# A Swin-style window attention block on one core: the copy of v split in two, and the narrow low parts of norm 2 moved ahead of the second half of the scores

## The reference, cut to what matters

```python
xn = layernorm(x, ln1_w, ln1_b)
xs = jnp.roll(xn, shift=(-3, -3), axis=(1, 2))          # shifted 7x7 windows, no mask
qkv = windows(xs) @ qkv_w + qkv_b                       # 6 heads of 32, 49 tokens a window
attn = softmax((q @ k.T) * hd ** -0.5)
x = x + unwindow((attn @ v) @ proj_w + proj_b)
h = layernorm(x, ln2_w, ln2_b)
h = gelu(h @ mlp_w1 + mlp_b1, approximate=False)        # 192 -> 768
x = x + (h @ mlp_w2 + mlp_b2)                           # 768 -> 192
```

## Time and profile before

| | value |
|---|---|
| median of the timed runs | 3025.48 us |
| the profiled execution, its own time | 3029.68 us |
| its span, first to last instruction | 3027.8 us |
| mean granted clock of TensorE, share of full speed | 0.995 |
| TensorE busy | 2994.0 us (99%) |
| weight loads busy | 2832.8 us (94%) |
| VectorE busy | 2376.4 us (78%) |
| ScalarE busy | 2302.3 us (76%) |
| GpSimd busy | 1672.7 us (55%) |

### The profile page before, as it was taken

How to read it: one execution, slowest core, us unless ns; L and a number is a source line. 1 busy time by engine, 2 the same in 40 slices (tenths; PEclk the granted TensorE clock), 3 DMA queues, 4 the chain that set the end, 5 groups by cost and what they waited for, 6 DMA issues and landing times.

```text
span 3027.8 us, 114959 instructions
## 1 busy us (share of the span) xinstructions
PE 2994.0 (99%) x43446; PEld 2832.8 (94%) x43446; DVE 2376.4 (78%) x6418; ACT 2302.3 (76%) x4493; POOL 1672.7 (55%) x1934
## 2 busy tenths in 40 slices
PE   7999999999999999999999999999999999999998
PEld 6999999999999999999999999999999999999997
DVE  5887888788778877887788788878877887788775
ACT  4777777777777777777777777777777777777776
POOL 3555555555555555555555555555555555555553
PEclk8999999999999999999999999999999999999999
DMA  1110001001100100010001000100110010001000
GB/s 47 28 29 25 24 26 29 24 24 27 29 24 24 29 26 24 24 30 26 24 25 30 25 24 26 29 24 24 27 29 24 24 29 26 24 24 30 26 25 18
DMA packets 109326, 79.79 MB, mean 26 GB/s; under 512 B 7294, under 2 KB 108782, under 8 KB 109294
## 3 DMA queue, kind: packets, MB, share of 16 engines
q1 hardware_dynamic: 107682, 77.18, 9.4%
q10 hardware_dynamic: 1612, 2.16, 0.2%
HBM read 40.78 MB, written 38.54 MB: 26 GB/s over the span
## 4 chain that ended last, share of the span: by engine, by line
PE 98%; DVE 1%; ACTq 1%; ACT 0%; issue 0%; POOL 0%; DVEq 0%; POOLq 0%
PE ps L836 36%; PE ps L839 16%; PE ps L913 6%; PE ps L945 5%; PE ps L867 5%; PE ps L918 5%; PE ps L964 5%; PE ps L919 4%; PE ps L914 4%; PE ps L915 4%; PE ps L799 3%; PE ps L807 2%; PE ps L929 2%; PE ps L933 1%; PE ps L809 1%
## 5 line engine op out<-in xcount | busy, mean ns | idle before, releaser
L390 POOL TENSOR_TENSOR gl<-g,gh 128x392 fp32r<-128x392 f32 x768 | 788.4, 1049 | 251.1 <-ACT gh L684 250.3
L836 PE MATMUL ps<-zh,w 128*128 128x392 f32 x3072 | 722.7, 350 | 0.6 <-ACT zh L646 0.6
L836 PEld LDWEIGHTS ps<-zh,w 128*128 128x128 f32 x3072 | 532.8, 188 | 65.3 <-ACT vt L672 39.8
L275 POOL TENSOR_TENSOR prob<-prob,rcp 128x588 f32<-128x588 f32 x128 | 152.6, 1192 | 529.6 <-DVE rcp L575 529.6
L424 DVE BATCH_NORM_STATS2 st<-xin 98x6 f32<-98x192 f32 x512 | 145.9, 348 | 321.8 <-DMA xin<-in_x 321.6
L678 ACT ACTIVATE g<-ps,biasf 128x392 f32<-128x392 f32 x768 | 389.9, 575 | 2.9 <-PE ps L836 2.9
L363 POOL TENSOR_TENSOR xb<-xin,projbv 98x768 f32<-98x768 f32 x128 | 234.8, 1834 | 271.3 <-DVE z L437 265.2
L684 ACT ACTIVATE gh<-g 128x392 fp32r<-128x392 f32 x768 | 364.6, 533 | 0.0
L836 PE MATMUL ps<-zh1c,wqkv 128*128 128x392 f32 x1536 | 360.9, 343 | 2.6 <-DVE zh1c L447 2.6
L696 ACT ACTIVATE yn<-ps,cols 64x392 f32<-64x392 f32 x128 | 74.9, 585 | 281.2 <-PE ps L919 281.2
L913 PE MATMUL ps<-gh,w2h 128*128 128x392 f32 x768 | 287.7, 375 | 0.2 <-ACT pt L761 0.2
(11 more groups left out here) (110 smaller groups left out, 7290.8 us busy)
## 6 DMA issues: line engine op xcount, KB each, us to landing
xin<-in_x SPq DMA_DIRECT2D x128, 147.0 KB
out<-yo SPq DMA_DIRECT2D x128, 147.0 KB
xin<-in_x SPq DMA_DIRECT2D x128, 71.2 KB
out<-yo SPq DMA_DIRECT2D x128, 71.2 KB
xin<-in_x SPq DMA_DIRECT2D x128, 54.8 KB
out<-yo SPq DMA_DIRECT2D x128, 54.8 KB
xin<-in_x SPq DMA_DIRECT2D x128, 18.8 KB
out<-yo SPq DMA_DIRECT2D x128, 18.8 KB
```

The source lines that it names most:

```text
L390: pool.tensor_tensor(gl[:, m, :], g[:, m, :], gh[:, m, :].bitcast(F32), ALU.subtract)\
L836: last = pe.matmul(dst, cols(w, part), act_, start=(n == 0), stop=(n == 4))
```

## The change

Three things are done.

- The one copy of v from two PSUM banks (L672, 768 columns) becomes two copies of one bank each (384 columns). The first stands ahead of the first exponential, the second between the two exponentials, where the whole copy stood. The matmuls of v signal each bank when it is ready.
- Chunk 2 of `mlp1` waits for the first copy alone, and chunk 3 for the second. The other users of `v_done` and `v_ready` count two where they counted one.
- On VectorE, `low_narrow2` goes from behind `scores(i, 1)` to ahead of it, straight behind `low_wide2`.

```diff
             def pad_windows(grp):
-                wait(pool, v_done, 1, grp - 1, 1)
+                wait(pool, v_done, 2, grp - 1, 2)
...
                 if feeds(i):
                     low_wide2(prev)
+                    low_narrow2(prev)
                 if attends(i):
                     scores(i, 1)
-                if feeds(i):
-                    low_narrow2(prev)
...
-            def values(i):
+            def values(i, pairs):
-                wait(act, v_done, 1, i, 1)
+                wait(act, v_done, 2, i, pairs + 1)
                 wait(act, pv_done, 1, i - 1, 1)
-                act.activation(vt[:, :, :], ps[0:PAIR + 1, V:V + 2, :].rearrange("p b (q n) -> p (b q) n", n=256)[:, :, 0:C],
+                act.activation(vt[:, 2 * pairs:2 * pairs + 2, :],
+                               ps[0:PAIR + 1, V + pairs, :].rearrange("p (q n) -> p q n", n=256)[:, :, 0:C],
                                ACT.Copy).then_inc(v_ready, 1)
...
                 if attends(i):
+                    values(i, 0)
                     exponential(i, 0)
-                    values(i)
+                    values(i, 1)
                     exponential(i, 1)
...
-                last.then_inc(v_done, 1)
+                    if p % 2:
+                        last.then_inc(v_done, 1)
...
-                    if m == 2 and attends(prev + 1):
-                        wait(pe, v_ready, 1, prev + 1, 1)
+                    if m >= 2 and attends(prev + 1):
+                        wait(pe, v_ready, 2, prev + 1, m - 1)
...
             def turn_probs(i):
-                wait(pe, v_ready, 1, i, 1)
+                wait(pe, v_ready, 2, i, 2)
```

## The result

The changed kernel takes 3098.61 us (median of 4 runs, 3097.75 to 3098.9), the kernel before 3025.22 us (median of 4, 3024.63 to 3027.86): a ratio of 1.0237, 95% interval 1.0224 to 1.0250. It is slower by 73.4 us. Between the two profiled executions the difference is 3098.62 - 3029.68 = 68.9 us, since the one of before lies 4.5 us above its median; what follows from the traces is to be held against 68.9, or 0.543 us in each of the 127 bodies.

What follows compares the result with a forecast made beforehand. TensorE was taken as the bound, beside a loop through three engines: a 0.88 us delay less 0.23 us slack gives +0.65 us in each of 127 bodies, about +83 us on 3025.5, so 3108 us; range 3079 to 3115.

Steps and rivals of the forecast that it cites:

- The copy of v hidden, each half 0.5 us: ScalarE, around the first exponential: two copies of 0.5 us cost nothing, hidden in idle time; at most 0.2 us otherwise.
- TensorE's two stops gone, 0.40 us: `mlp1`: stops ahead of chunk 2 (0.25 us) and passes 3 and 4 (0.15 us) go; TensorE reaches `turn_probs` 0.40 us earlier.
- the wait in half 1 alone: TensorE's transposes: half 1 (L945), due at about 1503.39, waits for GELU until 1503.65.
- The second subtraction and exponential 0.88 us later: VectorE, then ScalarE: the moved narrow pair delays `scores(i, 1)` and the second exponential by 0.88 us, the high end.
- My low bound of 0.65: VectorE: if the moved pair overlaps its neighbours, the scores shift by 0.65 us, giving 3079 us.
- ScalarE's chain has 0.23 us of slack there: At the MLP's first output matmul (L913): it could have started at 1504.36 but started at 1504.59.
- each as soon as the one in front is done: ScalarE, second exponential to copies of the transposed probabilities: each instruction starts once its predecessor ends, with no idle time.
- All move by 0.88 us: ScalarE behind the second exponential: table load, GELUs, high parts and copies of the probabilities are all 0.88 us later.
- my 0.05 us: From the end of ScalarE's first copy of the probabilities to L913: a released instruction starts 0.03 to 0.05 us later.
- Rival (a), faster: ScalarE's chain not delayed; TensorE's 0.40 us gain cut to the 0.23 us slack: 29 us gained, 2996 us; chance 0.09.
- Rival (c), part of the delay made up between exponential and copies: ScalarE makes up about 0.3 us of the delay, so 44 us slower, 3070 us; chance 0.07.
- Rival (d), the attention output late for `proj`: Ahead of L774, 0.05 us left isn't enough: a further 0.1 to 0.2 us a body, 3121 to 3134 us; chance 0.07.

Runs made afterwards that it cites:

- e2: Changed kernel with `low_narrow2` put back behind `scores(i, 1)`, so only the copy of v is split: 3024.30 us, ratio 0.9998 to the kernel before.
- e4: Changed kernel with both narrow low parts kept in partitions 0 to 63 and written to a scratch tile: 3050.31 us, ratio 1.0084 to the kernel before.
- e5: Kernel before with v's copy split and `mlp1` passes 0 to 2 of chunk 5 moved ahead, narrow parts unmoved: 2984.95 us, ratio 0.9865.
- e6: Kernel before with only `mlp1` passes 0 to 2 of chunk 5 moved ahead, v copied by one instruction: 3011.62 us, ratio 0.9953.
- e1: Kernel before with only `low_narrow2` moved ahead of `scores(i, 1)`, v copied by one instruction: 3095.46 us, ratio 1.0235.
- e3: Changed kernel with the second narrow low part put back behind the second half of the scores: 3047.76 us, ratio 1.0074 to the kernel before.
- e7: Changed kernel with `mlp1` passes 0 to 2 of chunk 5 moved ahead: 3099.18 us, ratio 1.0241 to the kernel before.

## Why the prediction was right, and which term was off

The forecast was 3108 us, +83; measured is +73.4 (+68.9 between the profiled executions). Step by step:

- The copy of v hidden, each half 0.5 us: right, 0.49 us in ScalarE's idle time. The first exponential starts at 7.94 us from the residual, before at 7.85; nobody waits for it, as the prediction had it. e2 shows that the split is free.
- TensorE's two stops gone, 0.40 us: right, it was 0.37. L947 starts at 13.90 us from the residual, before at 13.98. It would have started at 13.61 (0.36 us behind the last pair at 1511.46), but its weight load waits 0.46 us there. I had expected the wait in half 1 alone; it is in both halves, since GELU of chunk 1 is late as well. It costs nothing, as L915 is later still.
- The second subtraction and exponential 0.88 us later: right to the hundredth. The reason, that L461 neither overlaps its neighbours nor is overlapped, was shown in e4, which got 0.36 of the 0.88 back. My low bound of 0.65 was too high, by the overlap inside the pair.
- "ScalarE's chain has 0.23 us of slack there": this is the term that was mis-sized; it was 0.88 - 0.54 = 0.34. The step behind it is "each as soon as the one in front is done", and with it "All move by 0.88 us". Three things were wrong in it. The first copy didn't start as soon as the one in front was done: it waited for TensorE, worth 0.17 us when TensorE is early. Each copy took 0.662 us (median) before and 0.634 after, 0.03 less. And the way from the copy's end to the matmul is longer than my 0.05 us: 1513.74 + 0.63 = 1514.37 to 1514.51, 0.14, so 0.09 us of the slack wasn't there. The rows held a sign of this: the narrow parts end at 1499.36 and the passes that need them start at 1499.51, 0.15 later. 0.23 + 0.17 + 0.03 - 0.09 = 0.34. With it the sum is 127 x 0.54 = 69, against 68.9 between the profiled executions. Here 0.09 of the error in the slack hid part of the other 0.20; without it the forecast would have been further off. e5 and e4 agree with the larger slack: in e5 L917 is 0.36 us earlier where 0.23 would have allowed 29 us of gain, not 42, and e4's shift of 0.52 costs 25 us where 0.23 would give 127 x 0.29 = 37.
- The remaining 4.5 us between 68.9 and 73.4 is the distance of the profiled execution of before to its median. The prediction took 4.2 us off, as if the changed kernel's profiled execution would also lie above its median; it lies on it (3098.62 and 3098.61). So in terms of the profiled executions the forecast was 3113 against 3098.6, 14 us too high (127 x 0.11), and it is luck that only 9 of them are left between the medians.
- Rival (a), faster: e5 has its condition, a shift of 0 with both stops gone, though reached by another edit, and gains 42 us where the rival said 29. By the traces the change would have lost nothing below a shift of about 0.34 us (0.23 in the prediction); no run has a shift between 0 and 0.48.
- Rival (c), part of the delay made up between exponential and copies: part of it was true. Of the 0.88 us, 0.17 are made up there, not 0.3, and not because ScalarE works faster but because a gap in its chain closes; the prediction had held against it that "the rows join without a gap".
- Rival (d), the attention output late for `proj`: not seen; ScalarE still waits for TensorE ahead of L775 in 62 bodies (12.9 us), so it is nearly level, as the prediction had it.

## What to carry to other kernels

When a stop of the busiest engine is removed by reordering its supplier, follow what is pushed back on the supplier until it meets the busy engine again, and compare that delay with the slack at the meeting point; here 0.88 us against 0.34 at a place 6 us further on. It can be cheaper to give the waiting engine other work that is ready than to hurry what it waits for. And a slack read off a trace can hide the waiting engine's own lateness: ask of each instruction in the chain whether it starts by overlapping the one in front or after a gap.

## What the runs showed of the hardware

- Two VectorE instructions of 64x196 elements that read one half of the partitions and write the other take 0.76 us from the first's start to the next instruction; two of the same size that stay in partitions 0 to 63, and write to a tile of their own, take 0.54 us: they overlap each other and the next (e4).
- A copy of 128x588 from PSUM by ScalarE took 0.660 to 0.662 us (median of 256) in the kernel before, in e2 and in e6, and 0.632 to 0.634 in the changed one and in e1, e3, e4, e5 and e7, with the same operands. The split isn't the reason: e2 has it and e1 hasn't. In the first three the copy starts from 0.05 us before to 0.08 after the end of the instruction in front, in the bodies read from the others 0.08 or 0.09 before it. The cause was not tested.
- A matmul that waited for ScalarE's copy started 0.14 us after its end at L915, where the one behind the copy of v started 0.05 us after (1498.22 to 1498.27). The passes behind the narrow low parts started 0.15 us after their end (1499.36 to 1499.51, and 1519.98 to 1520.13 in e2). Why they differ was not tested.
